# Delta stage of a vision-Mamba layer in 512-column pieces: own PSUM banks, two-stage delta projection, logarithm added on GpSimd

## The reference

```
x = x @ in_W                      # 64 -> 128 channels, L = 48*48 = 2304 positions
x = silu(depthwise_conv3x3(x) + conv_b)
x0 = x.reshape(B, Di, L);  x1 = x.transpose(0, 1, 3, 2).reshape(B, Di, L)
xs = [x0, x1, x0 reversed, x1 reversed]              # K = 4 directions
dts, Bmat, Cmat = split(einsum('bkdl,kcd->bkcl', xs, x_proj_W), [4, 20])
delta = softplus(einsum('bkrl,kdr->bkdl', dts, dt_W) + dt_b)
h = h * exp(delta * A) + (delta * xs) * B;  y = h . C   # 2304 steps in sequence
```

## Time and profile before

| | |
|---|---|
| time, median of 3 runs | 6581.43 us (6579.79 to 6591.75) |
| the profiled execution, its own time | 6577.67 us |
| its span, from first to last instruction | 6575.9 us |
| delta stage, from first image load to the scan stage's first instruction | 100.07 to 988.75 us |
| mean granted TensorE clock, whole span | 0.917 of 2.4 GHz |

### The profile page before, as it was taken

One profiled execution on the slowest core, in us unless ns is written; L12 is line 12 of the kernel. 1 busy time (PEld: TensorE's weight loads), 2 busy tenths in 40 slices (PEclk: granted clock), 3 DMA queues, 4 the chain that ended last, 5 costly groups with the idle time before them and its releaser, 6 DMA issues. The chain is left out here.

```text
span 6575.9 us, 86273 instructions
## 1 busy us (share of the span) xinstructions
PE 5383.8 (82%) x22548; PEld 3529.8 (54%) x22548; DVE 4385.1 (67%) x4337; ACT 3873.2 (59%) x7966; POOL 4109.4 (62%) x2729
## 2 busy tenths in 40 slices
PE   5767648999989899898998999955589999966994
PEld 2222215555555555555555555522269999944773
DVE  2455548999999999999999999967331211153332
ACT  2565557788778788778887888844532222232232
POOL 0233338999989999899998999942014444402441
PEclk7788879999999999999999999977789999975997
DMA  3344337777777777777777777765200000012213
GB/s 79 116 148 140 141 131 233 249 249 244 250 234 248 243 247 245 238 247 244 247 248 239 249 244 248 246 210 176 97 22 0 0 0 0 0 50 88 78 59 107
DMA packets 432423, 1073.25 MB, mean 163 GB/s; under 512 B 97545, under 2 KB 140586, under 8 KB 427386
## 3 DMA queue, kind: packets, MB, share of 16 engines
q1 hardware_dynamic: 420570, 1043.06, 48.9%
q0 software_dynamic: 7584, 20.72, 1.0%
q10 hardware_dynamic: 3840, 4.72, 0.3%
HBM read 883.38 MB, written 184.94 MB: 162 GB/s over the span
## 5 line engine op out<-in xcount | busy, mean ns | idle before, releaser
L852 POOL TENSOR_TENSOR scan_hc<-scan_h,scan_c_rep 128x768 f32<-128x768 f32 x1536 | 2745.3, 1828 | 282.1 <-PE scan_ps_y L683 220.2
L683 PE MATMUL scan_ps_y<-scan_hc,keep_ident 128*128 128x512 f32 (+1 forms) x6144 | 2221.9, 489 | 21.6 <-ACT scan_y L718 21.6
L817 DVE TENSOR_TENSOR_SCAN scan_h<-scan_da,scan_h,scan_ps_p 128x768 f32<-128x768 f32 x896 | 1573.4, 1795 | 0.0
L683 PEld LDWEIGHTS scan_ps_y<-scan_hc,keep_ident 128*128 128x128 f32 x6144 | 1070.2, 191 | 824.6 <-issue 740.6
L774 ACT ACTIVATE scan_da<-scan_dd,layer_a_neg 128x768 f32<-128x768 f32 x1344 | 1208.9, 925 | 195.9 <-DVE scan_h L817 190.3
L735 ACT ACTIVATE scan_warm<-scan_du_t 128x128 f32<-128x128 f32 x4032 | 1243.0, 388 | 2.5 <-PE scan_ps_p L674 1.9
L1194 POOL TENSOR_TENSOR attn_e_lo<-attn_e,attn_e_hi 128x384 fp32r<-128x384 f32 x432 | 438.2, 1014 | 773.1 <-DVE attn_e_hi L1185 773.1
L817 DVE TENSOR_TENSOR_SCAN scan_h<-scan_da,scan_ps_p 128x768 f32<-128x768 f32 x448 | 760.7, 1733 | 2.0 <-ACT scan_da L774 2.0
L796 DVE TENSOR_TENSOR scan_ps_p<-scan_ps_p,scan_dd 128x768 f32<-128x768 f32 x672 | 634.6, 944 | 137.2 <-PE scan_ps_p L666 135.7
L1185 DVE CAST attn_e_hi<-attn_e 128x384 fp32r<-128x384 f32 x432 | 165.3, 383 | 713.6 <-ACT attn_e L1173 713.6
L674 PE MATMUL scan_ps_p<-keep_ident,scan_warm 128*128 128x128 f32 x4032 | 580.5, 281 | 71.5 <-DVE scan_h L817 67.2
(11 more groups left out here) (279 smaller groups left out, 7483.2 us busy)
## 6 DMA issues: line engine op xcount, KB each, us to landing
scan_c_rep<-bc_dram SPq DMA_DIRECT2D x1536, 384.0 KB, 4.2
dd_dram<-delta_dd SPq DMA_DIRECT2D x96, 768.0 KB, 3.4
scan_dd<-dd_dram SPq DMA_DIRECT2D x96, 768.0 KB, 5.6
scan_b_rep<-bc_dram SPq DMA_DIRECT2D x192, 384.0 KB, 4.8
y_dram<-scan_y SPq DMA_DIRECT2D x96, 384.0 KB, 4.5
merge_y<-y_dram SPq DMA_DIRECT2D x32, 1152.0 KB, 10.6
delta_pad<-xn_dram SPq DMA_DIRECT2D x16, 576.0 KB, 27.3
xs_dram<-delta_xs SPq DMA_DIRECT2D x8, 1152.0 KB, 25.4
```

The lines of the kernel that those rows point to most:

```text
L683: mm = pe.matmul(ps_y[:, lo:hi], keep["ident"][:, :], hc[t % HR][:, lo:hi], start=n == 0, stop=n == N - 1)
L817: dve.tensor_tensor_scan(view(h[n]), view(x), view(y), start, ALU.mult, ALU.add).then_inc(scan_done, 1)
L852: pool.tensor_tensor(hc[t % HR][:, :], h[t % N][:, :], c_rep[t % CR][:, :], ALU.mult).then_inc(hc_done, 1)
```

## The change

- A group is one unit and a pair of directions (forward and reversed on the same data): 16 groups of 2 x 2304 columns, in 9 pieces of 512 (`IG = 9`). The middle piece straddles the two directions. Loops are written out.
- Projection and exponential have PSUM banks of their own: `ps_a` and `ps_e`, three banks each. `dt_W` as a stationary operand (cut in two parts, `w_dt` and `w_dt_lo`) replaces `w_eff`: `project` makes B, C and the four low-rank rows of both directions in one matmul of 96 outputs, six blocks of 384 a group, for the next group. ACT and DVE cut them into a high and a low part (`cut`, rows of ones carry the bias). `expand` then makes a piece of the delta projection by two float32r matmuls over 104 and 64 rows.
- ACT has no `Relu`: `Abs`, `Exp`, then three `Ln` of 1536 columns at the end of the group. `magnitude` (the `Abs`) of piece i+1 stands before the `Exp` of piece i.
- DVE makes `dm` into `du`, `e - dm` into `de`, and then `max(v, 0) + de` in one `scalar_tensor_tensor`, which is what frees `ps_a` (`v_done`). It shares the cutting of `ps_b` with ACT.
- POOL adds the logarithm (`add_log`) and multiplies by `x` (`drive`), 768 columns at a time, when the group's logarithms are there. It no longer makes the low part.
- Images have no border columns: the shifted taps of `convolve` write 47 of 48 columns. A block is cut into two halves of three matmuls, in pieces with i%3 = 0 and 1; `take_conv` stands in DVE's piece with i%3 = 1. Nine blocks and group 0's six projections stand ahead of the loop.
- SP stores `delta` and `delta * x` by a DMA each, B and C with their parts a group ahead. `setup_phase` fetches `dt_W` in eight DMAs of single elements behind a memset and cuts it in two.

```diff
+        late = [(dt_raw[40:41, :, :], w["dt_b"].rearrange("(a k) d -> a k d", a=1))]
+        for r in range(2):
+            for at in (32, 96):
+                for k in (2 * r, 2 * r + 1):
+                    late.append((dt_raw[at + R * r:at + R * r + R, k, :], w["dt_W"][k].rearrange("d r -> r d")))
...
+        SLOTS = (1, 2, 4, 5, 7, 8)
...
+        def conv_block(g, i):
+            u, p = divmod(g, PAIRS)
+            unit = u + 1 if p == 0 else u + 2
+            return (unit, (3 if p == 0 else 0) + i // 3) if unit < U else None
+        def proj_block(g, i):
+            return (g + 1, SLOTS.index(i)) if i in SLOTS and g + 1 < G else None
...
+            for g in range(G):
+                u, p = divmod(g, PAIRS)
+                if g:
+                    store_dd(g - 1)
+                if g + 1 < G:
+                    store_bc(g + 1)
...
+            def convolve(unit, t, first, last):
...
+                    pe.wait_ge(c_taken, unit * TPI + t)
...
+            def project(g, b):
...
+                if m:
+                    pe.wait_ge(lo_done, m)
+                    pe.wait_ge(even_taken, (m + 1) // 2)
+                x = xs[u % 3] if p == 0 else xt[u % 2]
+                pe.matmul(ps_b[0:6 * N, 0:TT], keep["w_bc"][:, p, :], x[:, b * TT:b * TT + TT], start=True, stop=True).then_inc(b_full, 1)
+            def expand(g, i):
+                n = g * IG + i
+                pe.wait_ge(hi_done, TPI * g + blocks_for(i))
+                pe.wait_ge(lo_done, TPI * g + blocks_for(i))
+                if n >= 3:
+                    pe.wait_ge(v_done, n - 2)
+                for r, at, a, b in spans(i):
+                    d = g % PAIRS + 2 * r
+                    pe.matmul(ps_a[n % 3][:, a:b], keep["w_dt"][:, d, :], cut[g % 2][:, at:at + b - a], start=True, stop=False)
+                    mm = pe.matmul(ps_a[n % 3][:, a:b], keep["w_dt_lo"][:, d, :], cut[g % 2][0:64, at:at + b - a], start=False, stop=True)
+                mm.then_inc(a_full, 1)
...
+            for g in range(G):
+                for i in range(IG):
+                    expand(g, i)
+                    if proj_block(g, i):
+                        project(*proj_block(g, i))
+                    if conv_block(g, i) and i % 3 < 2:
+                        convolve(*conv_block(g, i), 3 * (i % 3), 3 * (i % 3) + 3)
...
+            def take_block(g, b):
+                m = TPI * g + b
+                act.wait_ge(b_full, m + 1)
...
+                if m % 2 == 0:
+                    act.activation(bc[g % 2][:, b * TT:b * TT + TT], ps_b[0:6 * N, 0:TT], ACT.Copy).then_inc(even_taken, 1)
+                act.activation(cut[g % 2][0:40, b * TT:b * TT + TT], ps_b[0:40, 0:TT], ACT.Copy).then_inc(hi_done, 1)
...
+            for g in range(G):
+                for i in range(IG):
+                    n = g * IG + i
+                    if n + 1 < G * IG:
+                        magnitude(n + 1)
+                    act.wait_ge(mag_done, n + 1)
+                    if n >= 3:
+                        act.wait_ge(co_done, n - 2)
+                    act.activation(ps_e[n % 3][:, :], mag[n % 3][:, :], ACT.Exp, scale=-1.0).then_inc(ex_done, 1)
+                    if i + 1 < IG and proj_block(g, i + 1):
+                        take_block(*proj_block(g, i + 1))
+                for r in range(LOGS):
+                    log(g, r)
+                if g % PAIRS == 0 and g // PAIRS + 1 < U:
+                    silu(g // PAIRS + 1)
...
+                    dve.wait_ge(ex_done, n + 1)
+                    dve.tensor_scalar(du[g % 2][:, at], ps_e[n % 3][:, :], 1.0, -1.0, ALU.add, ALU.add).then_inc(dm_done, 1)
+                    if i + 1 < IG and proj_block(g, i + 1):
+                        take_block(*proj_block(g, i + 1))
+                    dve.wait_ge(dm_done, n + 1)
+                    dve.tensor_tensor(de[g % 2][:, at], ps_e[n % 3][:, :], du[g % 2][:, at], ALU.subtract).then_inc(co_done, 1)
+                    if conv_block(g, i) and i % 3 == 1:
+                        take_conv(*conv_block(g, i))
+                    dve.wait_ge(co_done, n + 1)
+                    dve.scalar_tensor_tensor(de[g % 2][:, at], ps_a[n % 3][:, :], 0.0, de[g % 2][:, at], ALU.max, ALU.add).then_inc(v_done, 1)
```

More of the change, by code:

```diff
@@ L139, in _ @@
             pe.wait_ge(loaded, 16 * n_loads)
+            pe.wait_ge(ident_set, 1)
             for k in range(K):
[L142 to L147, removed]
+                mm = pe.transpose(ps_w[:, k, 0:R + 2 * N], x_rows[:, k, :], keep["ident"][0:R + 2 * N, 0:R + 2 * N])
             mm.then_inc(bc_ps, 1)
@@ L286, in delta_phase @@
[L286 to L293, removed]
@@ L341, in _ @@
+            store_dd(G - 1)
             for k in range(2):
[L342 to L345, removed]
+                sp.wait_ge(dd_out[k], 32 * CG * (G // 2))
+                sp.wait_ge(bc_out[k], 64 * (G // 2))
             for k in range(3):
[L347 to L350, removed]
+                sp.wait_ge(xs_out[k], 16 * ((U + 2 - k) // 3))
@@ L352, in _ @@
         @block.tensor
         def _(pe):
-            def convolve(unit, k, t):
+            def convolve(unit, t, first, last):
                 o = ps_c[:, 0:TT]
+                ov = o.rearrange("p (r w) -> p r w", w=W)
+                iv = img[unit % 2][:, :].rearrange("p (r w) -> p r w", w=W)
                 r0 = t * (TT // W)
[L358 to L363, removed]
@@ L386, in _ @@
-            pe.wait_ge(img_here[0], 32)
-            for t in range(TPI):
-                convolve(0, 0, t)
-            with pe.Fori(0, UP - 1) as i:
-                pair(i, False)
-            pair(UP - 1, True)
+                RB = TT // W
+                if first == 0:
+                    if t == 0:
+                        pe.wait_ge(img_here[unit % 2], 32 * (unit // 2) + 32)
+                    pe.wait_ge(c_taken, unit * TPI + t)
+                taps = [(dx, one) for dx in (1, 0, 2) for one in range(2)]
@@ new lines, in convolve @@
+                for n in range(first, last):
+                    dx, one = taps[n]
+                    a, b = max(0, 1 - dx), min(W, W + 1 - dx)
+                    if one:
+                        lhs, rows, x = keep["w_one"][:, dx, :], slice(r0 + 2, r0 + 2 + RB), iv[0:64]
+                    else:
+                        lhs, rows, x = keep["w_pair"][:, dx, :], slice(r0, r0 + RB), iv
+                    mm = pe.matmul(ov[:, :, a:b], lhs, x[:, rows, a + dx - 1:b + dx - 1], start=n == 0, stop=n == 5)
@@ new lines, in _ @@
+            for t in range(TPI):
+                convolve(0, t, 0, 6)
+            for t in range(3):
+                convolve(1, t, 0, 6)
+            pe.wait_ge(ones_set, 2)
+            for b in range(TPI):
+                project(0, b)
+            for g in range(G):
[5 more added lines that the diff above has]
+                        convolve(*conv_block(g, i), 3 * (i % 3), 3 * (i % 3) + 3)
@@ L409, in pair @@
-            def pair(i, last):
-                for k in range(2):
-                    unit = i * 2 + k
-                    for q, (d, c) in enumerate(order):
-                        j = (k * Q + q) % 3
-                        act.wait_ge(a_full, unit * Q + q + 1)
-                        act.activation(halves(mag[j]), ps_a[j][:, :, 0:HW_], ACT.Abs, bias=keep["dt_b"][:, d:d + 1]).then_inc(mag_done, 1)
-                        act.activation(halves(pos[j]), ps_a[j][:, :, 0:HW_], ACT.Relu, bias=keep["dt_b"][:, d:d + 1]).then_inc(mag_done, 1)
-                        act.wait_ge(mag_done, unit * (2 * Q) + 2 * q + 2)
-                        act.activation(ps_a[j][:, :, 0:HW_], halves(mag[j]), ACT.Exp, scale=-1.0).then_inc(ex_done, 1)
-                        if q % 3 == 2:
-                            for r in range(q - 2, q + 1):
-                                log(unit, k, r)
-                        if q == 8:
-                            cut(unit, 0)
-                    cut(unit, 1)
-                    if not (last and k):
-                        silu(unit + 1, (k + 1) % 2)
@@ new lines, in magnitude, with log @@
+            def magnitude(n):
+                act.wait_ge(a_full, n + 1)
+                act.activation(mag[n % 3][:, :], ps_a[n % 3][:, :], ACT.Abs).then_inc(mag_done, 1)
+            def log(g, r):
+                act.wait_ge(co_done, IG * g + 3 * r + 3)
+                x = du[g % 2][:, r * 3 * PIECE:(r + 1) * 3 * PIECE]
+                act.activation(x, x, ACT.Ln, bias=1.0).then_inc(ln_done, 1)
+            silu(0)
+            act.wait_ge(ones_set, 2)
+            for b in range(TPI):
+                take_block(0, b)
@@ L527, in scan_phase @@
+            turn(0)
+            for g in range(G):
+                for j in range(CG + 1):
+                    if j < CG:
+                        add_log(g, j)
+                    if j:
+                        drive(g, j - 1)
+                if g % PAIRS == 0 and g // PAIRS + 1 < U:
+                    turn(g // PAIRS + 1)
 def scan_phase(nc, P, keep):
```

324 lines of the change are left out of this document (154 added, 170 removed).

## The result

| | median | runs | ratio to before |
|---|---|---|---|
| before | 6580.61 us | 6576.82 to 6591.75 | |
| after | 6649.18 us | 6645.52 to 6660.57 | 1.0104 (95%: 1.0087 to 1.0122) |

The account below looks back on a forecast made before the run. Delta stage bounded by a chain of handovers, afterwards a wait loop through the convolution's PSUM bank: 39 rounds of 15.2 us, 593 us, plus setup and tail end it at 947, 42 us gained: 6539 us, range 6440 to 6620.

Parts of the forecast that it names:

- Which clock: PE's clock in the loop: two thirds of its work per three-piece round at 1.2 GHz, giving 15.2 us a round.
- the lower clock holds throughout: Rival: PE stays at 1.2 GHz, 78 us more, 6617 us; chance 0.24 together with rounds above 16.2 us.
- E: PE's `expand` of one piece, two float32r matmuls of 512 columns: 1.0 us at the lower clock, 0.56 at the higher.
- So I take rows for free: PE's matmuls: 104 or 64 rows cost the same time as 128, since `w_one` cost as much as `w_pair`.
- The round at the lower clock: Three pieces in the loop with PE at 1.2 GHz: 17.2 us, of which ACT and DVE together 4.1.
- C: PE's convolution block of six matmuls, made in two halves per round: 9.5 us at the lower clock, 5.05 at the higher.
- P: PE's `project`, one float32 matmul of 384 columns: 1.45 us at the lower clock, 0.84 at the higher.
- The loop of waits: PE's next convolution block waits through `Abs`, `Exp`, DVE's work and `take_conv` on one PSUM bank: 11.3 to 17.2 us a round.
- The time line: Delta stage laid out from setup through convolution, 39 rounds, last groups and tail: ends at 947 us, 42 us gained.
- Groups 13 to 15: Last groups of the delta stage, without convolution and bounded by DVE: 88 us, to 921 us.
- POOL's additions cost nothing: The 96 logarithm additions on POOL cost nothing while a group exceeds 23.8 us, except 10.7 us behind the last group.
- the other case: Judging the 96 additions by the engine-selection rule instead of the round: on POOL they cost 83 us more than on DVE.

Follow-up runs that it names:

- e1: Changed kernel with `w_one` zero-filled to 128 rows, so all six convolution matmuls of a block read 128 rows: 6429.32 us, 0.9775 of before.
- e13: Changed kernel with each convolution block's matmuls reordered, three of 128 rows first, then three of 64: 6464.35 us, 0.9831 of before.
- e5: Changed kernel with both `expand` matmuls zero-filled to 128 rows, `w_one` left at 64: 6508.42 us, 0.9902 of before.
- e3: Changed kernel with DVE's copy out of `ps_c` moved ahead of its wait for the same piece's exponential: 6572.97 us, 0.9988 of before.
- e6: Changed kernel with ACT's `Exp` of a piece ahead of the next piece's `Abs`: 6649.52 us, 1.0115 of before.
- e9: Changed kernel with the 96 logarithm additions on DVE instead of POOL, six at the start of the next group: 6667.63 us, 1.0138 of before.

## Why the prediction was wrong

- **The step that failed** is the one under "Which clock": "I put two thirds of PE's work in a round at 1.2 GHz: 11.3 + 2/3 x 5.9 = 15.2 us." All of it ran at 1.2 GHz. This is 2.0 us in each of 39 rounds, 78 us. The rival "the lower clock holds throughout" came true. The evidence was in the earlier trace rows, 60 us of dense alternating work at 0.50, and I let the dense P and `w_pair` outweigh it. That the rounds of e1 average 14.2 and those of e13 14.8 does not confirm 15.2: their matmuls are cheaper at both levels as well.
- **Why before had 0.86**: four matmuls of `w_eff` and two of `w_bc`, all over 128 rows, stood between two blocks there. The change replaces `w_eff` by E at 104 and 64 rows, which puts more changes of rows in PE's stream. That this is why before was high is argued. Shown is the one side: take changes out at either place (e1, e5, e13) and the clock rises. A kernel after with `w_eff` back was not tried.
- **"So I take rows for free"** was wrong beside it. Both kinds cost the same in the earlier trace rows, but because each stood next to the other: both are dearer for it, 0.84 against 0.65 at the higher level, 1.57 against 1.28 at the lower. E shows it too: the second E of the round takes 1.45 at the lower level, against the 1.0 of my sum and the 1.02 of e5, which fills its rows.
- **The round at the lower clock** was 17.2 by my sum and is 18.0. C, P and the first E are right (12.03 us from 226.13 to 238.16, forecast 11.95). The rest, from the second E to the next block, is 5.97 instead of 5.3: E up to `Abs` 1.55 for 1.2, ACT 1.13 for 1.3, DVE 3.29 for 2.8, in which 0.23 is a wait for ACT's half of the block. With straddling pieces (0.6 in two of six rounds) and the boundary (2.6 in one of six), 39 rounds and boundaries take 725 us against 683 by the lower-clock rival: 42 more, which is why 6649 lies above its 6617 and above the range.
- **The loop of waits** through `ps_c` was right, e3 gives 76 us for cutting it; its path through `Abs` and `Exp` was one of two (e6).
- **The time line**: convolution from 117.3 (forecast 118.5), first half block at 226.1 (228, though 209.6 + 17.6 makes 227.2), first `dm` at 234.6 (238), 123.5 us behind the last round (114), of it 25 us of tail (25). Groups 13 to 15 took 10 us longer than told.
- **POOL's additions cost nothing**: right for the loop, where POOL stands 518 us waiting for the logarithms. The 83 us that the prediction gave for the other case took 0.95 us for each on DVE; with the additions there the kernel is slower (e9), not faster.
- **Stages behind**: forecast 0, measured 3.5 us less.

The sum: 120 us in the rounds (78 + 42) and 9.5 behind them, less 2 by the earlier first half block, are the 128 by which the stage ended later than the forecast 947.

## What to carry to other kernels

Read matmuls from start to start: "94% busy" hid a stream in which each matmul cost 0.29 us more than between its like, and whose clock never rose. Keep matmuls of one row count together, or fill rows up with zeros, which cost no time in any of these runs beyond their noise and gave 54 us even to the kernel before. And before moving an elementwise operation between GpSimd and VectorE, ask where its inputs lie, since with two in SBUF each engine slowed the other here.

## What the hardware did that I had not expected

- Reordering six matmuls with the same work and rows took PE's granted clock from 0.50 to 1.00 ahead of the loop, and to 0.68 in it.
- Alternating 128 and 64 rows costs 1.57 instead of 1.28 us for 384 float32 columns at the lower clock and 0.84 instead of 0.65 at the higher. The weight loads start with their matmul there and 0.32 us ahead of it where rows are equal.
- A DVE addition of two SBUF operands goes from 0.95 to 2.55 us beside POOL, and POOL's multiplication from 1.80 to 2.51.
